# A two-stage channel gate over 32 samples: another order of stores and reloads, and two transposes ahead of the sums of x

## The reference, cut to what matters

```
v  = group_norm(x, 32 groups)          # per sample: mean and variance of 16 channels x 3136 pixels
r  = relu(v)
r  = where(max(r) - mean(r) < 0.5, 0, r)                 # per channel, over the pixels
bb = 1 - exp(-|max_over_channels(r) - mean_over_channels(r)|)    # per pixel
y  = bb * r
pooled = mean(y);  ymax = max(y)                          # per channel
c1 = sigmoid(pooled @ W1.T);  c3 = relu(pooled @ W3.T);  c3 = where(c3 < 1, 1.2, c3)
out = x + where(y < c1 * c3 * ymax, 0, y)
```

## Time and profile before

| | |
|---|---|
| Median of 3 runs | 1783.85 us (1779.1 to 1792.09) |
| Profiled execution | 1780.24 us, span 1778.4 us |
| TensorE matmul busy | 1303.4 us (73%) |
| VectorE busy | 1460.9 us (82%) |
| ScalarE busy | 1306.6 us (73%) |
| GpSimd busy | 610.6 us (34%) |
| Mean granted TensorE clock | 0.843 |
| DMA | 518.86 MB, mean 292 GB/s |

### The profile page before, as it was taken

The page is one execution under the profiler, slowest core; times in us unless marked ns, Lnnn a source line. Parts: engine busy times, 40 slices in busy tenths (PEclk is TensorE's granted clock), DMA queues, the critical chain, the costliest instruction groups (busy, mean ns, idle before and its releaser), DMA issues.

```text
span 1778.4 us, 45243 instructions
## 1 busy us (share of the span) xinstructions
PE 1303.4 (73%) x19616; PEld 1080.2 (61%) x19616; DVE 1460.9 (82%) x2192; ACT 1306.6 (73%) x1921; POOL 610.6 (34%) x446
## 2 busy tenths in 40 slices
PE   4888776788876778767688777678777688777761
PEld 3766655666665666655576655566655566656660
DVE  2588887988887988888888887888887887888987
ACT  5678777777787878777767787777787767777821
POOL 0043233443233444223443233443233442233430
PEclk8898888998888898888888888898878887888885
DMA  9259989999999899998989999989999988899973
GB/s 396 87 162 301 319 315 320 281 296 297 312 330 336 277 285 306 302 329 320 287 263 296 307 330 332 283 277 296 301 330 329 279 265 269 315 329 343 296 228 145
DMA packets 93418, 518.86 MB, mean 292 GB/s; under 512 B 10272, under 2 KB 10272, under 8 KB 93216
## 3 DMA queue, kind: packets, MB, share of 16 engines
q1 hardware_dynamic: 75360, 416.38, 58.4%
q0 software_dynamic: 17856, 99.56, 28.7%
HBM read 310.38 MB, written 205.52 MB: 290 GB/s over the span
## 4 chain that ended last, share of the span: by engine, by line
PE 29%; POOL 26%; ACT 22%; DVE 15%; issue 7%; DMA 1%; SPq 0%; DVEq 0%; ACTq 0%; POOLq 0%
POOL xs L778 23%; ACT rs L476 8%; PE ps_turn L286 7%; PE ps_gate L347 7%; ACT xs L476 7%; PE ps_gate L322 6%; PE ps_gate L294 6%; DVE xs L670 6%; ACT rs L451 5%; DVE rs L670 4%; DVE max_and_mean L622 2%; POOL rstd L757 2%; DMA xs<-in_x 1%; PE ps_gate L356 1%; DVE xs L737 1%
## 5 line engine op out<-in xcount | busy, mean ns | idle before, releaser
L622 DVE TENSOR_REDUCE max_and_mean<-ps_turn 128x2 f32<-128x1024 f32 x384 | 466.0, 1220 | 201.3 <-PE ps_turn L286 200.6
L286 PE MATMUL ps_turn<-ident,xs 128*128 128x128 f32 (+1 forms) x1600 | 358.8, 310 | 177.7 <-DVE max_and_mean L622 112.3
L769 POOL DMA_DIRECT2D xs<-in_x x124 | 111.6, 968 | 940.0 <-DVE xs L670 837.0
L778 POOL TENSOR_TENSOR xs<-xs,rs 128x1568 f32<-128x1568 f32 x124 | 433.3, 3531 | 1.9 <-DVE rs L670 1.9
L286 PEld LDWEIGHTS ps_turn<-ident,xs 128*128 128x128 f32 (+1 forms) x1600 | 204.5, 153 | 311.5 <-DVE max_and_mean L622 155.2
L312 PE MATMUL ps_gate<-ident,bb 128*128 128x128 f32 (+1 forms) x1600 | 273.4, 333 | 153.2 <-ACT bb L469 144.0
L425 ACT ACTIVATE scratch<-xs 128x3136 bf16<-128x3136 f32 x128 | 360.2, 2814 | 7.8 <-DMA xs<-in_x 2.8
L312 PEld LDWEIGHTS ps_gate<-ident,bb 128*128 128x128 f32 (+1 forms) x1600 | 249.6, 239 | 173.4 <-DVE ymax_parts L639 157.7
L286 PE MATMUL ps_turn<-ident,rs 128*128 128x128 f32 (+1 forms) x1600 | 341.3, 299 | 6.0 <-issue 6.0
L639 DVE CUSTOM_DVE_ANT_0 xs<-xs,ps_gate 128x768 f32<-128x768 f32 (+1 forms) x256 | 243.3, 959 | 45.1 <-PE ps_gate L312 45.0
L451 ACT ACTIVATE xs<-xs,shift,rstd 128x3136 f32<-128x3136 f32 x64 | 191.9, 2999 | 100.0 <-POOL shift L761 93.3
(11 more groups left out here) (80 smaller groups left out, 991.9 us busy)
## 6 DMA issues: line engine op xcount, KB each, us to landing
xs<-in_x SPq DMA_DIRECT2D x260, 784.0 KB, 13.7
out<-xs SPq DMA_DIRECT2D x256, 784.0 KB, 8.2
xs<-in_x POOLq DMA_DIRECT2D x124, 784.0 KB, 11.1
rs<-in_L_conv_W SPq DMA_DIRECT2D x2, 1024.0 KB, 18.7
```

The source lines that it names most:

```text
L286: mm = pe.transpose(ps_turn[0:w, n % 2, b - 2 * i, P * t:P * (t + 1)], r_tile(s, t)[:, P * b:P * b + w], ident[:, :])
L622: ins = dve.tensor_reduce(max_and_mean[:, 2 * i:2 * i + 2, 0], ps_turn[:, n % 2, :, :], AX.X, ALU.max)
L778: pool.tensor_tensor(o, o, half(r_tile(s - 1, t), h), ALU.add).then_inc(added, 1)
```

## The change

SyncE's list is put in the order of the tiles: the in-place halves are stored first, each store is followed closely by the reload of an earlier half, and tiles 2 and 3 come after. LOAD_ORDER, which is also the order of the squares and of the sums of x, becomes 0, 1, 2, 3. On TensorE fills 3 and 4 move from behind the sums of x to ahead of them. Nothing is added or removed.

```diff
-LOAD_ORDER = (2, 0, 1, 3)
+LOAD_ORDER = (0, 1, 2, 3)
@@ block.sync, one sample
-                store(s, 2, 0)
                 store(s, 0, 0)
                 store(s, 0, 1)
+                reload(0, 0)
+                store(s, 1, 0)
+                reload(0, 1)
+                store(s, 1, 1)
+                reload(1, 0)
+                store(s, 2, 0)
+                reload(1, 1)
                 store(s, 2, 1)
-                store(s, 1, 0)
-                store(s, 1, 1)
+                store(s, 3, 0)
                 reload(2, 0)
-                store(s, 3, 0)
-                reload(0, 0)
-                reload(0, 1)
                 reload(2, 1)
                 store(s, 3, 1)
-                reload(1, 0)
-                reload(1, 1)
                 reload(3, 0)
                 reload(3, 1)
@@ block.tensor, one sample
                 mean_rows_of(s)
                 if s > 0:
                     pe.wait_ge(logits_ready, s)
+                turn(s, 3)
+                turn(s, 4)
                 if s + 1 < B:
                     sum_x(s + 1, range(0, 2))
                 turn_means(s)
                 if s + 1 < B:
                     sum_x(s + 1, range(2, T))
-                turn(s, 3)
-                turn(s, 4)
                 if s + 1 < B:
                     group_stats(s + 1)
                 spread(s, 0)
```

## The result

| | before | after |
|---|---|---|
| Median | 1785.11 us (4 runs) | 1829.55 us (4 runs, 1820.19 to 1842.45) |
| Ratio | 1 | 1.0253, 95% interval 1.0170 to 1.0335 |
| Profiled execution | 1780.24 us, span 1778.4 | 1836.4 us, span 1834.6 |

The account below looks back on a forecast made before the run. Bound by the ring of waits inside one sample, no engine above 82%. Terms -3.5 + 31 + 1.5 - 3 = +26 us, less 2, give 1804 profiled, about 1806 us median; range 1758 to 1832.

Parts of the forecast that it names:

- The good sample: Sample without a TensorE stop: GpSimd's affine starts 0.3 us later; five such samples add +1.5 us.
- How many samples stop: TensorE waiting for an instruction block around the sums of x: 25 stopped samples of 30, where 17 were seen.
- What a stop costs: Delay from TensorE's stops: -3.5 us on the 17 old ones, +31 on 8 new ones, +1.5 on good samples.
- Stores and reloads: SyncE's new order fills idle DMA time in stopped samples, reloads end earlier: -3 us, ends 0 and -7.
- 0; a us per stop at the worst, +25: Cost of stores going out among accumulating DMAs to instruction block fetches: 0, at worst a us per stop, +25.
- SyncE starves the DMA engines: Rival, 5%: each reload waits right behind a moving store, DMA queues run empty, 5.4 us a sample, 1940 us.
- Count stays: Rival, 30%: TensorE's stops stay near 17 and each costs less; 1770 to 1781 us, time 1776.
- fills were the price: Rival, 18%: with fills 3 and 4 done a TensorE stop costs only 1.3 us; 1761 us profiled, up to 1747.
- the first rival: The 30% rival that TensorE's stops stay near 17, time 1776 us.
- Sum: Whole kernel: terms add to +26 us, less 2 for covered waits, +24 on the profiled 1780.24; median about 1806 us.

Follow-up runs that it names:

- e1: Kernel before with only fills 3 and 4 moved ahead of the sums of x, stores and reloads as before: 1797.82 us, ratio 1.0075.
- e2: Kernel before with only SyncE's new list of stores and reloads and the new tile order, fills behind the sums: 1831.47 us, ratio 1.0242.
- e3: Kernel before plus 23 pairs of weight load and matmul per sample, holding the block boundary at a harmless place: 1747.22 us, ratio 0.9748.
- e5: Kernel before plus the same 23 pairs per sample and 72 pairs once, fixing the block boundary at a harmful place: 1854.34 us, ratio 1.0379.
- e10: Kernel before with its late first store and tile order, but stores and reloads grouped by direction: ratio 1.0122.
- e6: As e2, but five stores ahead of the first reload and two to four stores between a store and its reload: 1815.06 us, ratio 1.0160.
- e9: As e2, with early first store, but stores and reloads in groups of one direction: ratio 1.0165.
- e7: As e2, but the last store moved ahead of the reloads of tile 2: 1816.86 us, ratio 1.0165.
- e12: Kernel before with only the two stores of tile 0 moved ahead of the first store of tile 2: 1774.18 us, ratio 0.9953.

## Why the prediction was right in sign and range, and wrong in its cause

- **The good sample, +0.3.** Right: 10.25 for 9.94 us.
- **How many samples stop: 25, before 17.** Too many: 20 in e1, the fills alone. The changed kernel has 24, but e2, which leaves the fills where they were, has 24 too, so that number is no proof of this term. That the place of the boundary makes the stop is borne out by e3 and e5; that just one block is asked for ahead is my reading of the traces. The Trainium skill (Runtime: NRT & Kernel Launch, Instruction fetch mechanics) calls the crossing mostly hidden; e5 minus e3 is 107 us, so in this kernel it is not.
- **What a stop costs: -3.5 + 31 + 1.5 = +29.** Wrong in size: e1 measured +13. The delays of the affine summed to 64 us, where I had 47 + 31 + 1.5 = 80. I had 25 stops of 2.4 us in the mean, and e1 has 20 of 2.0 us. The new stops near the edge were short. In e1:

```profile
1079.68 1.15 PE L322 MATMUL ps_gate<-xs,sel 128*32 128x112 f32 x34
1082.00 2.12 PE L322 MATMUL ps_gate<-xs,sel 128*32 128x112 f32 x78 [1.17 <-issue]
```

  1.2 us and the remaining 78 matmuls at full rate (2.12 us; 112 took 2.89 in the earlier trace rows), where I took 2.4 and 1.5 more for the clock. I had taken the mean stop and the clock loss of samples whose request came deep among the accumulating DMAs.
- **Stores and reloads: -3, ends 0 and -7, and their cost for instruction blocks "0; a us per stop at the worst, +25".** This is the step that failed: +43 measured by itself (e2). I had priced what the new list fills and put what it delays at nothing. TensorE's stops ahead of the sums grew from 33.3 to 56.9 us in e2, and squares and sums waited 42.8 us for loads; how far the two overlap I did not work out. "The moved issues are 8 stores and 8 reloads in either list" was true and beside the point. I gave the worst case to stores that go out early; e10 has none and its stops grew to 49.4 us. With the transfers no longer strictly in turn (e6, e9) some 29 of the 43 us remain.
- **The rival 'SyncE starves the DMA engines' (5%)** had the right place and a wrong mechanism. I argued against it that two transfers are always between a store and its reload; for two of the eight reloads, the first and the last of the list, it is one. Still the engines stayed busy for 0.93 to 0.97 of the time; e7, with the last store freed, took back a third. Its signs came: squares and sums wait for loads, last reload after the next accumulating DMAs. Its 1940 us was far off.
- **Count stays, fills were the price.** The count rose by 3, which is nearer to the first rival's 17 than to my 25, but its time (1776) did not come either: e1 was slower than before, not faster.
- **Sum.** +24 forecast, +44 (median) measured: 13 from the fills with 29 forecast, 43 from the list with -3 forecast. That the time lies in the range, 2 us below its upper end, is luck: two errors of opposite sign. (My forecast's own range ran to 1835, beyond the 1832 of the range as a whole; the two do not fit together.)

## What to carry to other kernels

When stores and loads share a DMA queue that is nearly always busy, look at GB/s beside the busy share before reordering them: the busy share hides a loss of rate, and a list strictly in turn, each reload close behind its own store, cost 7 to 8% of the packets' time here against a grouped list. When an engine with dense short instructions stops with no wait shown, count the instructions between stops; if they fall at multiples of one block, the length of the loop body decides where the stops fall, and a few added instructions can be a gain. And a kernel whose transfers end just as the next sample's begin has no slack for either: look at the samples that go well one by one, as the mean over all of them hid here where the loads ran over.

## What the runs showed of the hardware that I had not expected

- Packets of one queue with the same bytes took 1039 us before, 1048 to 1061 us in three other lists and 1124 to 1141 us with stores and reloads strictly in turn. Most of the difference is in some 650 to 850 packets of over 1 us among 66048 whose median is 239 ns.
- 46 instructions per sample more made the kernel 2.5% faster (e3), and the same 46 with the boundary at another place 3.8% slower (e5).
- Stores that share the DMA engines with accumulating DMAs did not lengthen the packets of the latter in sum: 508 us in e2, 510 before (27.8% of 1828.8 and 28.7% of 1778.4). But the last of the four landed 23.9 us after the first was issued, before 19.2. By itself that did not cost: in e12 it is 23.2.
